# First tiles of layer 1's FFN and of the MoE prepared inside the attention stages ahead of them

## The reference

```
x = x + tanh(g_xattn[l]) * attention_l(layernorm(x), ctx)
x = x + tanh(g_ffn[l])   * ffn_l(layernorm(x))
```

## Time and profile before

| | us |
|---|---|
| median of three runs (lowest, highest) | 1121.83 (1121.52, 1123.78) |
| the profiled execution: its own time | 1122.7 |
| the profiled execution: span from first to last instruction | 1120.9 |
| TensorE busy in it | 1057.9 |
| mean granted TensorE clock | 0.977 |

### The profile page before, as it was taken

The page is one execution under the profiler, slowest core; times in us unless marked ns, Lnnn a source line. Parts: engine busy times, 40 slices in busy tenths (PEclk is TensorE's granted clock), DMA queues, the critical chain, the costliest instruction groups (busy, mean ns, idle before and its releaser), DMA issues.

```text
span 1120.9 us, 18676 instructions
## 1 busy us (share of the span) xinstructions
PE 1057.9 (94%) x6238; PEld 905.3 (81%) x6238; DVE 788.3 (70%) x1809; ACT 518.2 (46%) x1196; POOL 165.2 (15%) x227
## 2 busy tenths in 40 slices
PE   5887899998999999999999998999989999999998
PEld 4765567776999978887888886999868888888887
DVE  5787879987788755558888866888556564565544
ACT  4666553343555555545554542556533334234232
POOL 2231000001111052230111001133322010010000
PEclk9899999999999989999999998999899999999999
DMA  9401010001000000000000005000022221121221
GB/s 284 103 1 41 1 12 1 1 1 75 1 0 0 1 12 1 1 1 1 1 0 0 1 1 240 1 0 1 1 58 70 64 75 54 57 80 48 67 85 29
DMA packets 30376, 41.22 MB, mean 37 GB/s; under 512 B 13615, under 2 KB 19577, under 8 KB 29414
## 3 DMA queue, kind: packets, MB, share of 16 engines
q1 hardware_dynamic: 29437, 39.63, 11.1%
q10 hardware_dynamic: 873, 0.72, 0.3%
HBM read 37.80 MB, written 2.54 MB: 36 GB/s over the span
## 4 chain that ended last, share of the span: by engine, by line
PE 51%; DVE 2%; ACT 1%; DMA 0%; issue 0%; DVEq 0%; POOL 0%; ACTq 0%; SPq 0%
PE psum L2023 16%; PE psum L2034 8%; PE psum L1398 6%; PE psum L1376 5%; PE psum L1213 3%; PE psum L1171 3%; PE psum L349 2%; PE psum L1386 2%; PE psum L1195 1%; PE psum L1184 1%; PE psum L1415 1%; PE psum L1995 1%; PE psum L1985 0%; PE psum L1407 0%; PE psum L1436 0%
## 5 line engine op out<-in xcount | busy, mean ns | idle before, releaser
L298 POOL TENSOR_TENSOR rstd<-ve,mhalf 128x1 f32<-128x1 f32 x128 | 84.2, 658 | 701.0 <-DVE ve L293 701.0
L360 ACT COPY work<-psum 128x256 f32<-128x256 f32 (+2 forms) x241 | 99.4, 438 | 141.0 <-PE psum L349 138.5
L349 PE MATMUL psum<-ident,work 128*128 128x128 f32 (+2 forms) x596 | 96.7, 284 | 15.0 <-DVE work L1352 3.2
L2108 ACT CAST h_hi<-work 128x512 fp32r<-128x512 f32 x68 | 42.2, 621 | 122.1 <-DVE work L2178 95.8
L2168 DVE TENSOR_TENSOR work<-psum,work 128x512 f32<-128x512 f32 x68 | 46.9, 690 | 72.3 <-ACT work L2100 72.2
L349 PEld LDWEIGHTS psum<-ident,work 128*128 128x128 f32 (+2 forms) x596 | 73.5, 148 | 29.5 <-DVE xT_lo L1300 5.6
L2023 PE MATMUL psum<-x_hi,ew_hi 128*128 128x512 f32 (+1 forms) x272 | 86.2, 398 | 0.2 <-ACT work L2100 0.2
L1597 PE MATMUL psum<-early,work 128*128 128x352 f32 x256 | 81.9, 475 | 3.3 <-ACT zone L572 2.8
L2023 PE MATMUL psum<-x_hi,ew_lo 128*128 128x512 f32 (+1 forms) x272 | 84.0, 390 | 0.0
L2023 PE MATMUL psum<-x_lo,ew_hi 128*128 128x512 f32 (+1 forms) x272 | 84.0, 390 | 0.0
L2034 PE MATMUL psum<-ew_hi,h_hi 128*128 128x256 f32 x272 | 76.2, 280 | 2.5 <-DVE h_lo L2185 2.4
(11 more groups left out here) (269 smaller groups left out, 2565.6 us busy)
## 6 DMA issues: line engine op xcount, KB each, us to landing
work<-expert_shares SPq DMA_DIRECT2D x64, 256.0 KB, 3.1
early<-in_experts_in SPq DMA_DIRECT2D x1, 6528.0 KB, 18.6
x<-in_x_in SPq DMA_DIRECT2D x4, 512.0 KB, 7.0
early<-in_W_in SPq DMA_DIRECT2D x2, 1024.0 KB, 5.9
out_x<-x SPq DMA_DIRECT2D x3, 512.0 KB, 4.4
early<-in_Wk SPq DMA_DIRECT2D x1, 1024.0 KB, 6.4
early<-in_Wq SPq DMA_DIRECT2D x1, 1024.0 KB, 8.9
zone<-in_Wv SPq DMA_DIRECT2D x1, 1024.0 KB, 13.2
```

What stands on the lines that cost most here:

```text
L298: pool.tensor_tensor(rstd[:, slot:slot + 1], ve[:, slot:slot + 1], mhalf[:, 0:1], ALU.pow).then_inc(s["rstd_ready"], 1)
L349: last = pe.transpose(dst[0:rows, at:at + n], src, ident[0:n, 0:n])
L360: act.copy(dst, src).then_inc(s["tr_copied"], 1)
```

## The change

For `ffn1` and `moe` the front work of group 0 leaves the head of the stage and goes into steps 13 to 17 of attention 1 and attention 3. The statistics go to steps 13, 14 and 15, the normalisation to steps 15 and 16, the transposes to steps 15 (tiles 0 and 1) and 16 (tiles 2 and 3), now into the score banks 0 to 2, the high parts to steps 15 and 17, the low parts to steps 16 and 17. The router logits of group 0 are made after step 17, before the barrier. The sixteen `keep_busy` matmuls go. Six of the sixteen pieces of the split of W1 and W2 go into steps 15 and 16 (ScalarE) and to the end of POOL's attention-1 stream, and ScalarE's wait for the load of W1 and W2 goes to step 3 of attention 1. In `ffn1` the buffer of high and low parts becomes two buffers by the parity of the group, so that the first one lies where attention 1 no longer uses anything; the second half of `x_lo` moves for the same reason.

```diff
-        def lead_group_vector(dve, s, first):
...
+        def front_turn(pe, l, j):
+            f = f_s[l]
+            pe.wait_ge(f["xn_ready"], j + 1)
+            pe.wait_ge(a_s[l]["s_read"], 3 * (T - 1) + j % 3 + 1)
+            wait(pe, f["tr_copied"], j - 2)
+            for k in range(KD):
+                last = pe.transpose(front_bank(j)[:, k * P:(k + 1) * P], xn[j % 2][:, k * P:(k + 1) * P], ident[:])
+            last.then_inc(f["tr_filled"], 1)
+        def front_high(act, l, j):
+            f = f_s[l]
+            act.wait_ge(f["tr_filled"], j + 1)
+            act.copy(front_parts(l, j)[0], front_bank(j).rearrange("p (a b) -> p a b", a=KD)
+                     ).then_inc(f["x_hi_done"], 1)
+        def front_low(dve, l, j):
+            f, (hi, lo) = f_s[l], front_parts(l, j)
+            dve.wait_ge(f["x_hi_done"], j + 1)
+            dve.tensor_tensor(lo, front_bank(j).rearrange("p (a b) -> p a b", a=KD), hi.bitcast(F32),
+                              ALU.subtract).then_inc(f["tr_copied"], 1)
+        def front_apply(dve, l, j):
+            ln_apply(dve, j, j, f_s[l], xn[j % 2]).then_inc(f_s[l]["xn_ready"], 1)
...
 att_tensor, step(t, p):
                 if has(t - 2):
                     project(t, on_unit)
+                if isinstance(t, int) and t == T - 1:
+                    front_turn(pe, l, 0)
                 if has(t + 1):
                     queries(1 - p, xn_unit)
                 if has(t - 1):
                     values(t, p, units)
+                if isinstance(t, int) and t == T - 1:
+                    front_turn(pe, l, 1)
+                if isinstance(t, int) and t == T:
+                    for j in range(2, GT):
+                        front_turn(pe, l, j)
...
             pipeline(pe, -1, step, [(tr, 2 * UNITS)], T + 1, AHEAD)
+            if l == 3:
+                router_logits(pe, 0)
             end_stage(pe, "pe")
 att_scalar, step(t, p), after the exponentials:
+                if isinstance(t, int) and t == T - 1:
+                    front_high(act, l, 0)
                 if l == 3 and (not isinstance(t, int) or 4 <= t < 4 + LAST_SPLIT):
                     split_scalar(act, "experts", t - 4)
+                if l == 1 and isinstance(t, int) and T - 1 <= t <= T:
+                    for n in (range(2) if t < T else range(2, W12_LEAD)):
+                        split_scalar(act, "W12", n)
+                if isinstance(t, int) and t == T - 1:
+                    front_high(act, l, 1)
+                if isinstance(t, int) and t == T + 1:
+                    for j in range(2, GT):
+                        front_high(act, l, j)
 att_vector, step(t, p):
-                if isinstance(t, int) and t >= T:
-                    lead_group_vector(dve, f_s[l], t == T)
+                if isinstance(t, int) and t == T:
+                    for j in range(2):
+                        front_low(dve, l, j)
+                    for j in range(2, GT):
+                        front_apply(dve, l, j)
+                if isinstance(t, int) and t == T + 1:
+                    front_low(dve, l, 2)
...  (after shift(1))
+                if isinstance(t, int) and t == T - 1:
+                    front_apply(dve, l, 0)
                 if has(t):
                     shift(2)
...
+                if isinstance(t, int) and T - 3 <= t < T:
+                    for j in {T - 3: (0,), T - 2: (1, 2), T - 1: (3,)}[t]:
+                        ln_stats(dve, j, j, f_s[l])
+                if isinstance(t, int) and t == T - 1:
+                    front_apply(dve, l, 1)
...  (after the residual)
+                if isinstance(t, int) and t == T + 1:
+                    front_low(dve, l, 3)
 att1_pool:
-            lead_group_pool(pool, f_s[1])
+            for j in range(GT):
+                ln_root(pool, j, j, f_s[1])
+            for n in range(W12_LEAD):
+                split_pool(pool, "W12", n)
 ffn1_tensor:
-            for j in range(GT):
-                group_transposes(pe, s, tr, j, j)
-                keep_busy(pe, 2)
 moe_tensor:
-            for e in XT_AT:
-                side(0, e)
-                keep_busy(pe, 2)
-            side(0, LG_AT)
             gate_up(0, 0, (0,))
             side(0, BT_AT)
```

More of the change, by code:

```diff
@@ L327, in led, with front_bank, front_parts @@
             return isinstance(t, int) and t < 2
-        def lead_group_vector(dve, s, first):
[L331 to L340, removed]
+        def front_bank(j):
+            return bank[j % 3][:, 0:D]
+        def front_parts(l, j):
+            cols = slice(j * P, (j + 1) * P)
+            hi, lo = (xg_hi[0], xg_lo[0]) if l == 1 else (x_hi, x_lo)
+            return hi[:, :, cols], lo[:, :, cols]
+        def front_turn(pe, l, j):
[18 more added lines that the diff above has]
+            ln_apply(dve, j, j, f_s[l], xn[j % 2]).then_inc(f_s[l]["xn_ready"], 1)
         def transposes(pe, s, tr, blocks, banks):
@@ L1138, in roots_pool @@
                         split_pool(pool, behind, 2 * i + p - start - 2)
-            for n in range(T - start - 2, pieces) if behind else ():
+            for j in range(GT if then is f_s[3] else 2):
+                ln_root(pool, j, j, then)
+                if behind and j == 0:
+                    split_pool(pool, behind, T - start - 2)
+            for n in range(T - start - 1, pieces) if behind else ():
                 split_pool(pool, behind, n)
-            (lead_group_pool if then is f_s[3] else lead_pool)(pool, then)
             end_stage(pool, "pool")
@@ L1839, in down, with group @@
                     last.then_inc(s["h_used"], 1)
-            def group(g, at, front, first=False):
+            def group(g, front, first=False):
                 pe.wait_ge(s["tr_copied"], tr.n)
                 for m in range(NM1):
-                    up(g, at, m, first)
+                    up(g, m, first)
                     if m >= 2:
@@ L1884, in unit, with group @@
                 act.copy(r_hi[m % 2][:], rf[m % 2]).then_inc(s["hi_done"], 1)
-            def group(g, next_at, front, pieces=lambda m: ()):
+            def group(g, front, pieces=lambda m: ()):
                 for m in range(NM1):
@@ L1973, in weights, with router_logits @@
             return part[:, at:at + D] if which == 2 else part[:, at + k * EH:at + (k + 1) * EH]
+        def router_logits(pe, g):
+            pe.wait_ge(f_s[3]["gw_ready"], 1)
+            pe.wait_ge(f_s[3]["tr_copied"], 7 * g + GT)
+            cols = bass.ds(g * 512, 512)
+            passes = [(w, a, k) for w, a in ((gw_hi, x_hi), (gw_hi, x_lo), (gw_lo, x_hi)) for k in range(KD)]
+            for n, (w, a, k) in enumerate(passes):
+                last = pe.matmul(bank[5][0:NE, :], w[:, k, :], a[:, k, cols], start=n == 0,
+                                 stop=n == len(passes) - 1)
+            last.then_inc(f_s[3]["tr_filled"], 1)
         def moe_tensor(pe):
             s, tr = f_s[3], Count()
+            tr.base = GT + 1
             def side(g1, e):
@@ L1988, in side @@
                 if e == LG_AT:
-                    if isinstance(g1, int) and g1 == 0:
-                        pe.wait_ge(s["gw_ready"], 1)
-                    pe.wait_ge(s["tr_copied"], tr.n)
-                    cols = bass.ds(g1 * 512, 512)
-                    passes = [(w, a, k) for w, a in ((gw_hi, x_hi), (gw_hi, x_lo), (gw_lo, x_hi)) for k in range(KD)]
-                    for n, (w, a, k) in enumerate(passes):
-                        last = pe.matmul(bank[5][0:NE, :], w[:, k, :], a[:, k, cols], start=n == 0,
-                                         stop=n == len(passes) - 1)
-                    last.then_inc(s["tr_filled"], 1)
+                    router_logits(pe, g1)
                     tr.up()
@@ L2131, in side @@
             def side(g1, e):
-                if e - 1 in XT_AT:
+                lead = isinstance(g1, int) and g1 == 0
+                if e - 1 in XT_AT and not lead:
                     t = g1 * GT + e - 3
```

82 lines of the change are left out of this document (39 added, 43 removed).

## The result

The changed kernel takes 1111.87 us (median of five runs, 1109.02 to 1115.46) beside 1121.83 us for the kernel before on the same chip (five runs, 1120.67 to 1125.46): a ratio of 0.9909 [0.9895, 0.9922]. The forecast was 1116.6 us with a range from 1112.8. The sign was right, the size was not: the gain is 10.0 us and not 5.2.

A forecast was written before the change was run, and what follows sets the result against it. It took engine-to-engine chains at the two seams, where TensorE is not dense, as what could be shortened. Savings of 2.7 and 2.5 us, together 5.2, off 1121.83 gave 1116.6 us, range 1112.8 to 1119.6.

The forecast's parts named there:

- What bounds the seams: Attention 1 to `ffn1`, attention 3 to `moe`: engine-to-engine chains, not load; 5.06 and 4.97 us from barrier to useful matmuls.
- TensorE in step 15: Two transposes ahead of `values` delay all that follows by 0.25 us; VectorE's 1.67 us wait is the cover.
- The end of step 17: Tile 3's low part, behind the last residual and before the barrier, adds 0.40 us, bounds 0.34 to 0.9.
- The clock term: W1's first products start at 1.2 GHz for 3.4 us, half lost: 1.7 us; ends nothing and 3.15.
- rival A: Transposes fill the last steps' waits, so the clock stays up: about 4 us more per seam, 1108.5 us; chance 0.07.
- seam 1: Attention 1 to `ffn1`: W1 4.41 us earlier, less 1.7 for the clock, gives 2.7 us, between 1.25 and 4.4.
- a clock of 1.00 in steps 16 and 17: Sign named in advance, in the attention tails, that would make the forecast wrong downwards; no size given.
- Seam 2: Attention 3 to `moe`: transposes of the logits 2.5 us earlier, ends 1.1 and 4.0 us.
- upper bound for the cold start: Behind attention 1's barrier: clock rising only after 6.3 us, as at attention 3's head, 3.15 us lost.
- B: The tail pays: VectorE or high parts late, 1 us more at each seam, 3.2 us gained, 1118.6 us; chance 0.11.
- C: Clock stays at 1.2 GHz through `ffn1`'s first group and `moe`'s first experts: 3.2 us slower, 1125.0 us; chance 0.05.
- D: Nothing gained: `moe`'s weight chain through DRAM does not move, a late root or high part eats the rest; 1121.5 us; chance 0.04.

The follow-up runs named there:

- e16_after: The changed kernel as it is, run again for a second profile; 1111.87 us, ratio 0.9911 to the kernel before.
- e5_turns: The kernel before plus four transposes of the identity, without use, behind `values` in step 16 of attention 1 and 3; 1119.17 us, ratio 0.9964.
- e12_late: The changed kernel with the transposes of tiles 2 and 3 moved from step 16's wait to behind step 17's projection; 1118.63 us, ratio 0.9956.
- e1_seam1: The changed kernel with attention 3 and `moe` as before, but `x_lo` at its new place; 1118.33 us, ratio 0.9962 to the kernel before.
- e7_x6984: The changed kernel with the second half of `x_lo` at word 6984 instead of 8408; 1111.79 us, ratio 0.9905 to the kernel before.
- e13_x7168: The changed kernel with the second half of `x_lo` at word 7168 instead of 8408; 1110.77 us, ratio 0.9885 to the kernel before.
- e8_hold_x8400: The changed kernel with `x_lo`'s second half at word 8400 and matmuls without use in the waits of attention 1 and 3; 1112.73 us, ratio 0.9918.

## Why the prediction was wrong, step by step

**What bounds the seams** was right: chains, shortened as read. In `e16_after` nothing of the head of `ffn1` is left but the wait at the barrier, 0.96 us, and the first four W1 products take 6.32 us as before.

**TensorE in step 15:** the next transposes come 7.57 us after the scores of step 15 where it was 7.35: 0.22 us for the 0.25 forecast. VectorE kept its cover; in front of the division it still waits 0.56 us for TensorE, which is the 1.67 of before less the 1.1 that the text reckoned with.

**The end of step 17:** the low part costs 0.41 us (forecast 0.40). High parts, roots and split pieces delayed nothing.

**The clock term is the step that failed.** The text said that at each seam the clock falls as before and half of 3.4 us is lost behind the barrier, and it gave rival A, the clock that stays up because transposes fill the waits, 0.07. In the profiled execution of the changed kernel, the cold start cost 7.86 - 6.32 = 1.54 us, the forecast's 1.7. But the tail ran 0.69 us shorter (18.55 to 17.86 from the scores to W1 or the barrier) where 0.65 more was expected: 0.94 us from step 17's projection at full clock, the rest from step 16 and the row behind the projection. So seam 1 gave 4.2 us for 2.7. At seam 1 A happened whole in seven of nine traces: 7.0 us, and A's price was right (2.7 + 4 = 6.7). The prediction named this sign itself, a clock of 1.00 in steps 16 and 17. Seam 2 is the same: from the logits to their transposes 4.68 us where 4.71 was worked out, so barrier and order of work were right, but the logits start 17.89 us after step 15's scores and not 19.14, 3.8 us for 2.5, and 6.5 with the clock up, which is so in four of nine traces. What misled was that the argument against A weighed how short the transposes are. The trace offered another reading: the falls, at 390.1 and 396.9, come 1.2 and 0.6 us behind the ends of two waits of 0.81 us each, so the wait is what there is to fill. (The prediction put the first fall at 390.4; a mean of 0.56 in the slice means 390.1.) `e5_turns` and `e12_late` show that for the second wait. Why the first fall comes in some executions and not in others stays open.

The prediction's upper bound for the cold start, 6.3 us at the head of attention 3, was not a start that a barrier made cold. In the trace of before the clock fell at 676.8, in the tail of attention 2, and stayed at 0.50 for 10.2 us.

The Trainium skill, TensorE: Matmul & The Clock Gate, Part 4 (PE-mode transpose), says that a transpose does not count as busy for the clock in the way a matmul does. By that rule `e5_turns` would equal the kernel before, 1122.95 us in those runs; it measured 1119.17. In this kernel, where the wait is between dense stretches, the rule does not hold, and the measurement decides. The rows call a transpose a MATMUL, so they don't show whether it ran in the mode that the page speaks of.

**The head of attention 3,** whose length the prediction left as it was, was cold in the trace of before and warm in both traces of the changed kernel: 383.5 to 380.6, 2.9 us. Over the 18 traces eight have about 380.6 and eight about 383.5, and the latter stands in some of the changed code too (`e1_seam1`, `e7_x6984`, `e13_x7168`, `e8_hold_x8400`). It differs by execution; that the change makes the warm case likelier wasn't shown.

**`x_lo`'s move was costed at nothing** by being left out of the sum: an edit that only gives an address. It costs 3.0 us.

**The account.** By the profiled pair: 0.7 later at the start, -4.2, -2.9, -3.8, -0.1, +3.0: -7.2 us, 1120.9 to 1113.7. By the mean over the traces without filling (nine for each seam, eight with both seams changed for the head of attention 3): -6.4 at seam 1, -5.4 at seam 2, -1.9 at the head of attention 3, +3.0 in `moe`: -10.7, beside -10.0 in the medians. Had only `x_lo` been missed, the kernel would have been slower than forecast. The omissions had opposite signs, so it is luck that the time came out as near to the forecast as it did: without the 3.0 us it would be 3 us further off. B, C and D did not happen: no cold stretch behind a barrier was longer than 3.4 us in the traces of the changed kernel.

## What to carry to other kernels

Where the clock falls in a tail of short waits, price the filling of each wait as a gain of its own, from the rows at half clock behind it, before pricing the move. Cost every edit, one that only shifts a buffer too: compare the lengths of the matmuls that read it before and after. Here distances between the buffers that were multiples of 256 words were the fast ones. And take more than one trace before a stretch at half clock is called a property of the program.

## What had not been expected of the hardware

Matmuls of 512 columns took 389 ns with every part of `x_lo` at a multiple of 256 words of its zone, and 392 to 396 ns with half of it at words 6984, 8400 or 8408, in the products that read only `x_hi` as well.

With four transposes of the identity (0.63 us) in the second wait of 0.81 us, the clock was at 1.00 behind it at both seams, where in the kernel before it fell 0.6 us behind the wait's end at the first; eight of them in the whole program made it 4.0 us faster.

The same program had none of its seams' falls in one execution and four of them in another, 6.2 us apart in span, with equal waits.

In eight of the 18 traces, and in neither of the changed kernel's nor in that of the kernel before, the clock also fell within 1.5 us of the first down product, at the end of the wait in front of it (2.44 us before, 2.25 in the changed kernel). Where it lasted longest, 6.8 us in `e5_turns`, the stretch to the end took 289.0 us in place of 286.4.
